# Attention with 16 distance heads, last unit: weighted values tile by tile, row sums from two half sums, third stack ahead of its gates

## The reference, cut to what matters

```python
def _L0_attn_ref(X, W_in, b_in, W_out, b_out):
    ...
    Q, K, V, G = jnp.split(P, splits, axis=-1)
    W = jnp.power(EPS + _cdist(Q, K), -P_POW)
    W = W / (EPS + jnp.sum(W, axis=-1, keepdims=True))
    A = jnp.einsum('hbts,hbse->hbte', W, V)
    H = G * A
    ...
    return H @ W_out + b_out

def _forward(hs, ...):                       # L0_ffn
    ...
    scores = jnp.einsum('bhsk,bhtk->bhst', Q[..., :KPH], K) / math.sqrt(KPH)
    attn = jax.nn.softmax(scores, axis=-1)
    ao = jnp.einsum('bhst,bhtv->bhsv', attn, V)
    ...

x = x + _L0_attn_ref(_layernorm(x), ...)
x = x + _L0_xattn_ref(_layernorm(x), ctx_1024, ...)
x = x + _L0_ffn_ref(_layernorm(x), ...)
```

## Time and profile before

| what | value |
|---|---|
| median of 3 runs | 1234.87 us (1234.72 to 1236.56) |
| the profiled execution: own time, span | 1234.61 us, 1232.8 us |
| mean granted clock of TensorE in it | 0.96 of full |
| busy: PE, DVE, ACT, POOL | 1118.1, 883.2, 881.9, 585.7 us |

### The profile page before, as it was taken

How to read it: one execution, slowest core, us unless ns; L and a number is a source line. 1 busy time by engine, 2 the same in 40 slices (tenths; PEclk the granted TensorE clock), 3 DMA queues, 4 the chain that set the end, 5 groups by cost and what they waited for, 6 DMA issues and landing times.

```text
span 1232.8 us, 17091 instructions
## 1 busy us (share of the span) xinstructions
PE 1118.1 (91%) x6103; PEld 576.1 (47%) x6103; DVE 883.2 (72%) x1735; ACT 881.9 (72%) x1156; POOL 585.7 (48%) x426
## 2 busy tenths in 40 slices
PE   6999999999999999998888898789998799998747
PEld 3344444444444444433233332277776577654435
DVE  6776677766766677656988978546745776766897
ACT  2999999999989998993666767754554677664422
POOL 2877777777767777595454635003331100000023
PEclk9999999999999999997889989999998899999879
DMA  7200000000000000020000000000001000000000
GB/s 173 71 1 1 1 1 1 1 1 1 1 1 1 1 1 1 1 70 1 19 1 1 1 1 1 2 1 1 1 1 65 1 1 2 1 1 1 1 10 26
DMA packets 25695, 14.24 MB, mean 12 GB/s; under 512 B 14622, under 2 KB 24588, under 8 KB 25484
## 3 DMA queue, kind: packets, MB, share of 16 engines
q1 hardware_dynamic: 25612, 13.15, 4.0%
HBM read 12.09 MB, written 1.05 MB: 11 GB/s over the span
## 4 chain that ended last, share of the span: by engine, by line
PE 34%; POOL 28%; DVE 18%; issue 16%; ACT 3%; POOLq 0%; DMA 0%; DVEq 0%; ACTq 0%
DVE ARENA L1181 6%; POOL ARENA L2805 6%; POOL ARENA L2803 6%; POOL ARENA L2799 6%; PE PS L1052 5%; POOL ARENA L2829 3%; POOL WQ L2816 3%; PE PS L922 3%; PE PS L1436 2%; PE PS L1026 2%; PE PS L854 2%; PE PS L1460 2%; PE PS L1427 2%; PE PS L870 2%; POOL WQ L2812 2%
## 5 line engine op out<-in xcount | busy, mean ns | idle before, releaser
L2655 DVE TENSOR_SCALAR ARENA<-PS,ARENA 128x512 f32<-128x512 f32 x256 | 171.6, 742 | 49.9 <-PE PS L2289 49.5
L1181 DVE TENSOR_REDUCE ARENA<-PS 128x1 f32<-128x512 f32 x256 | 160.8, 682 | 29.4 <-PE PS L870 28.9
L1097 ACT ACTIVATE ARENA<-PS 128x1024 f32<-128x1024 f32 x128 | 128.9, 1026 | 57.6 <-PE PS L908 57.3
L2473 ACT ACTIVATE ARENA<-ARENA 128x2048 f32<-128x2048 f32 x64 | 121.9, 1911 | 48.0 <-DVE ARENA L2655 47.4
L2289 PE MATMUL PS<-ARENA 64*128 64x512 f32 x512 | 137.2, 634 | 0.0
L2480 ACT ACTIVATE ARENA<-ARENA,consts_sb 128x2048 f32<-128x2048 f32 x64 | 124.7, 1995 | 0.4
L2299 PE MATMUL PS<-ARENA 128*64 128x512 f32 x512 | 118.6, 605 | 1.5 <-issue 1.5
L2486 ACT ACTIVATE ARENA<-ARENA 128x2048 f32<-128x2048 f32 x64 | 118.4, 1899 | 0.0
L1362 POOL TENSOR_TENSOR ARENA<-ARENA 128x512 f32<-128x512 f32 x32 | 40.7, 1271 | 121.4 <-DVE ARENA L1320 120.9
L870 PE MATMUL PS<-ARENA 32*128 32x512 bf16 x256 | 73.0, 409 | 20.4 <-DVE ARENA L1181 15.2
L2631 DVE TENSOR_SCALAR ARENA<-PS 128x512 f32<-128x512 f32 x32 | 22.1, 691 | 96.8 <-PE PS L2264 96.8
(11 more groups left out here) (313 smaller groups left out, 2536.5 us busy)
## 6 DMA issues: line engine op xcount, KB each, us to landing
ARENA<-in_window_bias_dram SPq DMA_DIRECT2D x1, 1536.0 KB, 6.6
WKVG<-in_L_attn_W_in_dram SPq DMA_DIRECT2D x3, 384.0 KB, 6.4
X<-in_x_dram SPq DMA_DIRECT2D x4, 256.0 KB, 3.8
W<-in_L_ffn_w_dram SPq DMA_DIRECT2D x1, 1024.0 KB
out_dram<-X SPq DMA_DIRECT2D x4, 256.0 KB, 2.3
BV<-in_L_attn_b_in_dram SPq DMA_DIRECT2D x1, 512.0 KB, 6.2
Wout<-in_L_attn_W_out_dram SPq DMA_DIRECT2D x1, 512.0 KB, 4.9
WQ<-in_L_attn_wq_dram SPq DMA_DIRECT2D x1, 512.0 KB, 3.3
```

Source lines behind the costliest of these rows:

```text
L1097: act.activation(PT[m % PT_SLOTS], bank(("cP", m)), ACT.Exp, scale=0.5).then_inc(sem("c_exp"), 1)
L1181: dve.tensor_reduce(NMX[:, w % 2, t, h:h + 1], bank(("cS", n, j)), AX.X, ALU.max, negate=True).then_inc(sem("c_max"), 1)
L2473: act.activation(chunk(u, half), chunk(u, half), ACT.Sqrt).then_inc(sem("rooted"), 1)
L2655: dve.tensor_scalar(D[:, u % 2, kt, hd, :], bank(("S", u, c)), K2[:, u % 2, kt, hd:hd + 1], 1e-30, ALU.add, ALU.max).then_inc(sem("guarded ...
```

## The change

Three things. TensorE takes the four tiles of unit 31's weighted values at steps 6 to 9, one a step, and the row sums at step 10. The row sums no longer wait for GpSimd's last addition: ones are multiplied by WSUM and by WPAIR, and the two add up in the bank. GpSimd leaves that addition out and makes the third stack ahead of unit 31's gates. Window 0's maxima are split at step 8, not 7, and unit 31 is gated at step 14, not 13.

```diff
-TAIL = {... "gated30": 5,  "sums31": 6, "logits2": 12, "gated31": 13, ...
+TAIL = {... "gated30": 5, "values31": 6, "split0": 8, "sums31": 10, "logits2": 12, "gated31": 14, ...
...
         if n == TAIL["sums31"]:
-            jobs += weighted_values_job(UNITS - 1, "cV4") + row_sums_job(UNITS - 1, "cP")
+            jobs += row_sums_job(UNITS - 1, "cP")
+        if n == TAIL["values31"]:
+            jobs += weighted_values_job(UNITS - 1, "cV4")
...
-                if at_window(n, 7) is not None:
+                if at_window(n, 7):
                     split_maxima(at_window(n, 7))
+                if n == TAIL["split0"]:
+                    split_maxima(0)
...
-            for w in range(2, WINS):
+            for w in range(3, WINS):
                 stack(pool, w)
...
-            def weighted_values(u):
+            def weighted_values(u, tiles=range(QT)):
                 pe.wait_ge(sem("v_sb"), u + 1)
-                o = begin(("PV", u))
-                for kt in range(QT):
+                o = begin(("PV", u)) if 0 in tiles else bank(("PV", u))
+                for kt in tiles:
...
             def row_sums(u):
-                pe.wait_ge(sem("w_summed"), u + 1)
+                last = u == UNITS - 1
+                if last:
+                    pe.wait_ge(sem("w_paired"), 2 * u + 2)
+                else:
+                    pe.wait_ge(sem("w_summed"), u + 1)
                 o = begin(("RS", u))
                 for hd in range(2):
                     mm = pe.matmul(o[hd * 64:hd * 64 + 64, :], const("ones")[:, 0:64], WSUM[:, u % 2, hd, :],
-                                   start=True, stop=True)
+                                   start=True, stop=not last)
+                    if last:
+                        mm = pe.matmul(o[hd * 64:hd * 64 + 64, :], const("ones")[:, 0:64], WPAIR[:, hd, :],
+                                       start=False, stop=True)
...
+                if 0 <= n - TAIL["values31"] < QT:
+                    weighted_values(UNITS - 1, (n - TAIL["values31"],))
                 if n == TAIL["sums31"]:
-                    weighted_values(UNITS - 1)
                     row_sums(UNITS - 1)
...
                 pool.tensor_tensor(WPAIR, D[:, u % 2, 2], D[:, u % 2, 3], ALU.add).then_inc(sem("w_paired"), 1)
+                if u == UNITS - 1:
+                    return
...
+                if u == UNITS - 1:
+                    pool.wait_ge(sem("c_tmx"), 1)
+                    stack(pool, 2)
                 scale_gates(u)
-            pool.wait_ge(sem("c_tmx"), 1)
             full(pool, ("RS", UNITS - 1))
```

More of the change, by code:

```diff
@@ L133, in first_norm @@
     return b if 1 <= b < B else None
-TAIL = {"sums30": 0, "scores2": 1, "values0": 2, "gated30": 5,  "sums31": 6, "logits2": 12, "gated31": 13, "out2": 14, "add2": 15,
+TAIL = {"sums30": 0, "scores2": 1, "values0": 2, "gated30": 5, "values31": 6, "split0": 8, "sums31": 10, "logits2": 12, "gated31": 14, "out2": 14, "add2": 15,
         "pieces": 15, "rstd22": 16, "add3": 16, "rstd13": 18, "normal22": 18, "turn22": 19, "normal13": 20, "turn13": 21,
@@ L2300, in weighted_values @@
                                        D[:, u % 2, kt, hd, :], start=kt == 0, stop=kt == QT - 1)
-                done(mm, ("PV", u))
+                if QT - 1 in tiles:
+                    done(mm, ("PV", u))
             def row_sums(u):
-                pe.wait_ge(sem("w_summed"), u + 1)
+                last = u == UNITS - 1
[3 more added lines that the diff above has]
+                    pe.wait_ge(sem("w_summed"), u + 1)
                 o = begin(("RS", u))
```

## The result

| | median | runs | ratio to before |
|---|---|---|---|
| before | 1235.63 us | 10 (1229.14 to 1239.01) | |
| changed | 1240.3 us | 10 (1236.1 to 1244.15) | 1.0044, 95% interval 1.0022 to 1.0065 |

The change makes the kernel slower, as forecast: by 0.44% by the ratio of the runs (5.4 us), by 4.7 us between the two medians. The forecast was 3.4 us, about 0.28%. That lies in the interval, but 1240.3 lies above the range (1235.0 to 1239.9). The profiled execution took 1244.15 us, the slowest of its ten, with a span of 1242.4; four of the ten took 1241.9 us or more at a mean clock of 0.950 or 0.951, the other six 1236.1 to 1240.4 at 0.959 to 0.963, and the trace is of the first lot. It came to unit 30's gated values (L2679 now, L2666 before) at 557.54 us, where before had 554.34: 3.2 us of its 9.6 lie ahead of everything that was changed. So I count from there.

What follows compares the result with a forecast made beforehand. It took the chain that ended last, running through TensorE from window 0's first values, as the bound, so L922's delay delays the rest. 1234.6 + 3.5 − 0.1 = 1238.0, given as 1238.1 us; range 1235.0 to 1239.9.

Steps and rivals of the forecast that it cites:

- The place and the mechanism: Late row sums of unit 31 delay inverse, copies, stack and gates, and so window 0's first values (L922).
- VectorE's hole comes back: VectorE near step 11: the filled 6.55 us hole returns smaller, from 567.6 to 570.1.
- the four row-sum matmuls: TensorE at step 10: 1.94 us if both heads run together, at most 2.8.
- The half sums are worth nothing: GpSimd's third addition (2.36 us) is saved, but had long been off the path.
- The sizes up to the first values: Chain to L922, window 0's first values: 579.0 instead of 575.48, 3.5 us late.
- The row sums' inverse: ScalarE turns unit 31's row sums, which end 4.4 us later than before.
- The stack: GpSimd's third stack, ahead of the gates: 7.24 us, from 569.6 to 576.85.
- From L922 to step 16: TensorE without a stop behind the first values: 9.3 us as before, all but the last 2.3 at half clock.
- I take −0.1: Clock term for L922 to step 16: where full clock starts moves the stretch −0.5 to +0.1 us; −0.1 taken.
- the dearer row sums: TensorE's row sums of unit 31 in three double passes, 2.8 us, L922 4.4 us late; 1239 to 1240, within slower's 0.70.
- That the clock stays up: Rival: full clock back before L922, stretch about 5.6 us, step 16 at 584.6; 1234.4, no change; chance 0.13.
- That the gates are not what L922 waits for: Rival: VectorE's step 14 decides, L922 at 576.2; 1235.3, no change; chance 0.07.

Runs made afterwards that it cites:

- Experiment 2: Changed kernel with ScalarE's copies of the third window's heads ahead of the inverse of unit 31's row sums; ratio to before 0.9976.
- experiment 1: Changed kernel with GpSimd's order of before, unit 31's gates ahead of the third stack; ratio to before 1.0026.
- experiment 3: Kernel before with only the third stack moved ahead of unit 31's gates on GpSimd; ratio to before 1.0002.
- 5: Kernel before with only unit 31's row sums made as two half sums at their old place, step 6; ratio to before 1.0016.
- experiment 7: Changed kernel with GpSimd's third addition and the whole row sums of before, still at step 10; ratio to before 1.004.
- experiment 4: Changed kernel plus two unused f32 matmuls of 512 columns in TensorE's gap behind step 14's scores; ratio to before 1.0009.
- 10: Control for experiment 4: changed kernel with one unused f32 matmul of 64 columns at the same place and bank; ratio to before 1.0061.
- experiment 9: Changed kernel with head copies ahead of the inverse, unit 31 gated at step 13, gates ahead of the third stack; ratio 0.9944, median 1229.9 us.
- 6: Changed kernel with head copies ahead of the inverse and unit 31 gated at step 13 again; ratio to before 0.997.
- 8: Kernel of 6 plus one unused f32 matmul of 512 columns behind step 13's scores and one behind step 14's; ratio to before 0.9986.

## Why the prediction was right or wrong

**The place and the mechanism were right.** All of the loss up to the first values runs over the late row sums, the inverse, the copies, the stack and the gates. Experiment 2 takes the order on ScalarE away and the whole loss with it (20.40, before 21.14), experiment 1 takes the order on GpSimd away and 1.35 us of the 4.35, and 3 shows that the stack's place alone makes the first values only 0.6 us later. The step at which VectorE's hole comes back (2.12 us at step 11, 2.5 forecast), its wait for the gates (2.36, 2.7 forecast), the split (0.9) and the four row-sum matmuls (1.95 us, 1.94 forecast) came as laid out. The half sums are worth nothing (5 and 7), as was said.

**The sizes up to the first values were short.** The row sums' inverse came 4.9 us later than before, not 4.4: tile, projections, maxima and turned maxima each took 0.1 to 0.2 more than laid out, and these add up. The stack took 573.25 to 580.81, so 7.56 us and not 7.24: its third operation took 1.68 instead of 1.36 while VectorE's L2690, on its side, took 1.76 instead of 1.11. That makes the first values 25.49 − 21.14 = 4.35 us late, where the sum had 3.5.

**The step that failed** is "From L922 to step 16", with its "I take −0.1". The prediction expected half clock there, but took its length, and so that of the stretch, as in before. The stretch was 10.58 us and not 9.3, +1.3. In before 7.0 us of it were at half clock and in the changed kernel 9.6; experiment 4 removes all of it and 3.2 us with it, and 10 shows that the clock did it. So the clock's term was mis-sized: it is about a fourth of the delay at step 16 in the profiled executions, 4.35 + 1.28 = 5.6 us. With 5.6 instead of 3.4 the forecast would have been 1240.2. Two things bound this account. Why half clock lasted 9.6 us here and not 7.0 stays open: experiment 9 has the long stretch behind short waits, experiment 7 the short one behind a long wait. And each kernel has one trace, the changed kernel's being of its slowest execution, so that 5.6 us come so near to the 5.4 of the ratio is in part luck.

**The range** ended at 1239.9 because its upper end held the dearer row sums "and a little of the clock". The row sums were not dearer. Beside the mis-sized clock and the 0.85 us missing at the first values, the median of before itself was 0.8 us higher in ten runs than in the three shown.

**The rules weighed.** TensorE: Matmul & The Clock Gate of the Trainium skill, section "Why this matters for your kernels", asks for no long idle gaps between bursts. Experiment 4 against 10 agrees: the gap of 4.3 us filled, the granted clock behind it is 1.00 and not 0.50. But a long gap is not needed for half clock here: before fell to it at 568.8 us with no gap over 1.57 us in the 10 us ahead, and experiment 3 at 571.75 us with none over 0.84. The other section of that page of the Trainium skill, "Part 3: Packing small matmuls — row/col tiling", has matmuls start and end strictly in program order. By it the row sums would have been three double passes, as the prediction worked out; the trace has two pairs of pairs, 568.58 and 569.49, and the whole is over in 1.95 us. The measurement decides against it here.

**The rivals.** That the clock stays up did not happen by itself. It came back ahead of the first values when the gap was filled, and then the time was that of before (1.0009). But that rival's sum was not what happened: at full clock TensorE took 7.31 us to step 16 (583.02 to 590.33) and not 5.6, as halving the time at half clock leaves out the wait of 1.07 us for VectorE, and step 16 was still 2.4 us later than before; that the whole kernel's time came out the same lies behind step 16. That the gates are not what L922 waits for was wrong in the changed kernel and is what the first experiment makes of it; the first values then came at 24.14 and not at the 21.9 (576.2) of that rival, since the inverse was 1.5 us later than in the sum and VectorE's steps 11 to 14 took longer. Experiments 2, 6 and 9 are faster than before, but their step 16 is only 0.4 to 0.95 us earlier; how much of the rest the orders bring about is open.

**What stays open.** Not all of a difference at step 16 arrives at the end, and some arises behind it. From step 16 to the end of the last window's values the profiled executions took 216.8 us in before, 217.0 and 216.9 in 5 and 7, 218.9 in the changed kernel and in 1, 218.8 in 10, 215.2 in 8, and 211.4 to 213.7 in 2, 3, 4, 6 and 9. Their time at half clock there goes the same way: 27.3 us in before, 5 and 7, 34.1 in the changed kernel, 1 and 10, 13.7 to 20.5 in the others. So the gain of 2, 6 and 9 over before is for the most part less time at half clock behind the changed place. How much of that each order brings about, and how much is chance of the execution, I did not separate; the intervals of the ratios hold both.

## What to carry to other kernels

When a step is moved to fill a hole, follow its result through every in-order engine to what stands behind its readers there: here a copy that needed nothing of the row sums stood behind their inverse, and one line's place on ScalarE decided between 0.44% slower and 0.24% faster. Then give the clock a range and not a term near nothing: the same work behind the changed place took 7.73 us with no half clock and 9.7 to 11.1 with 6.6 to 9.8 us of it, and the idle time just ahead did not tell which. And a saved operation is worth something only where its end was waited for last.

## What the runs showed of the hardware that was not expected

The kernel before does not scatter around one time. Of its 35 runs beside experiments 1 to 4, 11 took 1227.6 to 1230.3 us and the other 24 took 1235.0 to 1239.2, none between (of 35 others, run with experiments 5 to 8, six lay between); the mean granted clock listed with them was 0.961 to 0.965 in the first lot and 0.956 to 0.960 in the second. The same program is granted the full clock for more or less of its time, and the times that go with it lie 0.7% apart, more than this change makes. The mean clock does not tell all of it: beside experiments 9 and 10 three runs took 1229.5 to 1229.6 us at 0.959. Medians of three runs tell little here.

In the four row-sum matmuls the program's order is head 0 by WSUM, head 0 by WPAIR, head 1 by WSUM, head 1 by WPAIR; the trace has both heads' WSUM passes 0.01 us apart (L2316, 568.58) ahead of both heads' WPAIR passes (L2319, 569.49). The four took 1.95 us. By these records neighbours in the queue were not needed for the two heads' matmuls to run together.
